# Four-scan phase: merge and gate as two 64-row products, biases from a row of ones

## What is computed

```python
def _s6(x, xw, xb, bcw, bcb, dw, db, yw, yb):
    u = _linear(x, xw, xb)
    bc = _linear(x, bcw, bcb)
    delta = _linear(x, dw, db)
    Bm, Cm = jnp.split(bc, 2, axis=-1)
    A_bar = jnp.exp(-jax.nn.softplus(delta))
    B_bar = (1.0 - A_bar) * Bm
    elems = (A_bar, B_bar * u)
    ...
    _, h = jax.lax.associative_scan(combine, elems, axis=1)
    y = Cm * h
    return _linear(y, yw, yb)
...
y_cat = jnp.concatenate([y1, y2, y3, y4], axis=-1)
y_merged = _linear(y_cat, mw, mb)
gate = jax.nn.sigmoid(_linear(y_cat, gw, gb))
out = _linear(y_merged * gate, ow, ob)
```

## Time and profile before

| | us |
|---|---|
| median of 3 runs | 4187.93 |
| lowest and highest run | 4185.85, 4194.3 |
| profiled execution, its own time | 4188.53 |
| its span, first to last instruction | 4186.8 |
| TensorE, VectorE, ScalarE, GpSimd busy | 3537.3, 2700.7, 2737.2, 1647.8 |
| four-scan phase, from 2602.6 to 3290 of the span | 687.4 |

### The profile page before, as it was taken

The page is one execution under the profiler, slowest core; times in us unless marked ns, Lnnn a source line. Parts: engine busy times, 40 slices in busy tenths (PEclk is TensorE's granted clock), DMA queues, the critical chain, the costliest instruction groups (busy, mean ns, idle before and its releaser), DMA issues. The chain is left out here.

```text
span 4186.8 us, 73185 instructions
## 1 busy us (share of the span) xinstructions
PE 3537.3 (84%) x20680; PEld 2087.7 (50%) x20680; DVE 2700.7 (65%) x4346; ACT 2737.2 (65%) x4888; POOL 1647.8 (39%) x1503
## 2 busy tenths in 40 slices
PE   5899999886778999999976587899998683999946
PEld 2688888643334444444432143444443242999922
DVE  2566666675089999999999375566666573111146
ACT  4455555486988989889864286777776593333346
POOL 0233333200478989889887300455555100000000
PEclk9999999998999999999999798999999896999979
DMA  4000000112566576675752221000000123000022
GB/s 94 22 15 14 15 14 14 24 48 65 140 182 187 139 200 166 176 196 136 204 148 68 73 49 44 16 15 15 16 15 12 27 59 81 6 11 12 12 50 53
DMA packets 208408, 296.61 MB, mean 71 GB/s; under 512 B 73950, under 2 KB 193934, under 8 KB 207506
## 3 DMA queue, kind: packets, MB, share of 16 engines
q1 hardware_dynamic: 199062, 285.59, 26.3%
q10 hardware_dynamic: 9216, 9.65, 1.0%
HBM read 193.01 MB, written 102.03 MB: 70 GB/s over the span
## 5 line engine op out<-in xcount | busy, mean ns | idle before, releaser
L1576 POOL TENSOR_TENSOR mam_hc<-mam_h,mam_cs 128x896 f32<-128x896 f32 x336 | 703.3, 2093 | 181.9 <-DVE mam_h L1541 79.1
L1541 DVE TENSOR_TENSOR_SCAN mam_h<-mam_a,mam_kept,mam_dbx 128x448 f32<-128x448 f32 x672 | 737.5, 1127 | 18.0 <-ACT mam_a L1427 16.9
L1308 PE MATMUL mam_ps_y<-mam_hc,mam_ident 128*128 128x448 f32 x1344 | 568.3, 556 | 130.5 <-POOL mam_hc L1576 130.3
L1962 POOL TENSOR_TENSOR scan_ch<-scan_h,scan_cs 128x392 f32<-128x392 f32 x256 | 348.3, 1376 | 552.4 <-DVE scan_h L1928 552.4
L1308 PEld LDWEIGHTS mam_ps_y<-mam_hc,mam_ident 128*128 128x128 f32 x1344 | 248.4, 192 | 430.8 <-POOL mam_hc L1576 222.3
L1427 ACT ACTIVATE mam_a<-mam_ft,mam_a_neg 128x448 f32<-128x448 f32 x672 | 409.4, 657 | 81.5 <-DVE mam_h L1541 80.7
L1528 DVE TENSOR_TENSOR mam_dbx<-mam_ps_u,mam_bs 128x448 f32<-128x448 f32 x672 | 380.8, 610 | 35.0 <-DMA mam_bs<-dram_bc 35.0
L756 POOL TENSOR_TENSOR att_prob<-att_prob,att_share 128x588 f32<-128x588 f32 x128 | 151.6, 1184 | 452.6 <-DVE att_share L941 452.6
L1928 DVE TENSOR_TENSOR_SCAN scan_h<-scan_turned_in,scan_start 128x392 f32<-128x392 f32 x192 | 252.1, 1330 | 27.9 <-ACT scan_turned_in L1847 26.5
L1802 PE MATMUL scan_ps_merged<-scan_ch,scan_w_merge 128*128 128x392 f32 x512 | 230.7, 532 | 45.6 <-POOL scan_ch L1962 43.6
L2052 PE MATMUL lstm_ps<-lstm_hs,lstm_w_h 128*128 (+1 forms) x1344 | 264.9, 352 | 0.0
(11 more groups left out here) (216 smaller groups left out, 7777.4 us busy)
## 6 DMA issues: line engine op xcount, KB each, us to landing
mam_taps<-normed SPq DMA_DIRECT2D x1008, 43.5 KB
mam_bs<-dram_bc SPq DMA_DIRECT2D x28, 896.0 KB, 14.2
mam_cs<-dram_bc SPq DMA_DIRECT2D x28, 896.0 KB, 16.6
mam_ft<-dram_steps SPq DMA_DIRECT2D x42, 448.0 KB, 4.8
normed<-f_staged SPq DMA_DIRECT2D x384, 38.1 KB
f_mixed<-mixed SPq DMA_DIRECT2D x384, 36.8 KB
dram_gs<-mam_gs SPq DMA_DIRECT2D x56, 224.0 KB, 2.3
mam_gt<-dram_gs SPq DMA_DIRECT2D x56, 224.0 KB, 2.7
```

The source lines that it names most:

```text
L1308: mm = pe.matmul(ps_y[p % 2][:, 0:MT], ident[:], hc[t % 2][:, i, :], start=False, stop=(t % 8 == 7 and i == 1))
L1541: dve.tensor_tensor_scan(h[:, n % 8, :], a[t % 3][:, i, :], dbx[:, i, 0:MT], kept[:, at:at + 1], ALU.mult, ALU.add).then_inc(scanned, 1)
L1576: pool.tensor_tensor(hc[t % 2][:], h[:, row:row + 2, :], cs[:, 2 * pair:2 * pair + 2, :], ALU.mult).then_inc(weighed, 1)
L1962: pool.tensor_tensor(out, hd, in_order(cs, 1 - half, d, t, p), ALU.mult).then_inc(weighed, 1)
```

## The change

- The merge weights become one 128-row tile per direction without zeros: rows 0 to 63 hold merge and gate columns for the first image, rows 64 to 127 gate and merge columns for the second. In place of a product for merge and one for gate over 128 rows, there is a product for each image over its 64 rows. Product 0 leaves merge on partitions 0 to 63 and gate on 64 to 127 of its bank, product 1 the other way round in another bank.
- So the gate activation becomes two of 64 partitions, which read one half of partitions and write the other, and the product with the gate becomes two of 64 partitions.
- A 25th input row of ones in `xin` carries the biases of the four projections. Four small DMAs write it once, and the DMA of the biases is gone.
- u is no longer evacuated. VectorE forms ub = u x rest with u read from PSUM, when the second of three evacuations is done, and drive = B x ub with B read from PSUM.
- C is evacuated by a copy, and TensorE waits for the drive before it projects again.

```diff
-        w_merge = buf.sbuf("w_merge", [P, 2, DIRS, P])
+        w_merge = buf.sbuf("w_merge", [P, DIRS, P])
...
+                for p in range(2):
+                    for image in range(2):
+                        row = 32 * image + C
+                        sp.dma_start(xin[p][row:row + 1], w["rl_ones"][:, 0, 0:ROWS]
+                                     ).then_inc(weights_in, 16)
...
-                        pe.wait_ge(sided, done(c - 1, 4))
-                        pe.wait_ge(multiplied, done(c - 1))
+                        pe.wait_ge(sided, done(c - 1, 3))
+                        pe.wait_ge(fronted, done(c - 1))
...
-                        for a, ps in enumerate((ps_merged, ps_gate)):
-                            mm = pe.matmul(ps[:, 0:N], w_merge[:, a, n, :], ch[p][:, n, :],
+                        for rows, ps in zip((IMAGE_0, IMAGE_1), ps_merged):
+                            mm = pe.matmul(ps[:, 0:N], w_merge[rows, n, :], ch[p][rows, n, :],
                                            start=(n == 0), stop=(n == DIRS - 1))
...
-                    act.activation(gate[p][:], ps_gate[:, 0:N], ACT.Sigmoid,
-                                   bias=merge_b[:, 1:2]).then_inc(sigmoided, 1)
+                    act.activation(gate[p][IMAGE_0], ps_merged[0][IMAGE_1, 0:N], ACT.Sigmoid,
+                                   bias=merge_b[IMAGE_1, 1:2])
+                    act.activation(gate[p][IMAGE_1], ps_merged[1][IMAGE_0, 0:N], ACT.Sigmoid,
+                                   bias=merge_b[IMAGE_0, 1:2]).then_inc(sigmoided, 1)
...
-                        act.wait_ge(projected, done(c - 1, 4) + 1)
-                        act.activation(us[p][:], ps_in[U][:, 0:N], ACT.Identity,
-                                       bias=biases[:, U:U + 1]).then_inc(sided, 1)
...
+                for rows, other in ((IMAGE_0, IMAGE_1), (IMAGE_1, IMAGE_0)):
+                    both = ps_in[0][rows, :].rearrange("i (a d o) -> i a d o", a=2, d=DIRS)
+                    dve.tensor_copy(w_merge[rows, :, rows], both[:, 0])
+                    dve.tensor_copy(w_merge[rows, :, other], both[:, 1])
...
-                    dve.scalar_tensor_tensor(prod[p][:], ps_merged[:, 0:N], merge_b[:, 0:1],
-                                             gate[p][:], ALU.add, ALU.mult).then_inc(gated, 1)
+                    dve.scalar_tensor_tensor(prod[p][IMAGE_0], ps_merged[0][IMAGE_0, 0:N],
+                                             merge_b[IMAGE_0, 0:1], gate[p][IMAGE_0], ALU.add,
+                                             ALU.mult)
+                    dve.scalar_tensor_tensor(prod[p][IMAGE_1], ps_merged[1][IMAGE_1, 0:N],
+                                             merge_b[IMAGE_1, 0:1], gate[p][IMAGE_1], ALU.add,
+                                             ALU.mult).then_inc(gated, 1)
...
+                        dve.wait_ge(sided, done(c - 1, 3) + 2)
+                        dve.tensor_tensor(ub[p][:], ps_in[U][:, 0:N], rest[p][:], ALU.mult
+                                          ).then_inc(multiplied, 1)
+                        dve.wait_ge(multiplied, done(c))
                         dve.wait_ge(projected, done(c - 1, 4) + 3)
-                        dve.wait_ge(sided, done(c, 4))
-                        dve.scalar_tensor_tensor(ub[p][:], ps_in[B_][:, 0:N],
-                                                 biases[:, B_:B_ + 1], us[p][:], ALU.add,
-                                                 ALU.mult).then_inc(multiplied, 1)
-                        dve.wait_ge(multiplied, done(c))
                         dve.tensor_tensor(ring(drive, half)[:, bass.ds((t * 2 + p) * N, N)],
-                                          ub[p][:], rest[p][:], ALU.mult).then_inc(fronted, 1)
+                                          ps_in[B_][:, 0:N], ub[p][:], ALU.mult
+                                          ).then_inc(fronted, 1)
```

More of the change, by code:

```diff
@@ L1664, in four_scan_phase @@
         xin = [buf.sbuf(f"xin{p}", [P, ROWS, PAD]) for p in range(2)]
-        us = [buf.sbuf(f"us{p}", [P, N]) for p in range(2)]
         rest = [buf.sbuf(f"rest{p}", [P, N]) for p in range(2)]
@@ L1680, in four_scan_phase @@
         ps_in = [buf.psum(f"ps_in{i}", [P, BANK]) for i in range(4)]
-        ps_merged = buf.psum("ps_merged", [P, BANK])
-        ps_gate = buf.psum("ps_gate", [P, BANK])
+        ps_merged = [buf.psum(f"ps_merged{image}", [P, BANK]) for image in range(2)]
         ps_out = buf.psum("ps_out", [P, BANK])
@@ L1722, in stages @@
             tail(pairs * K - 1, 1)
+        IMAGE_0, IMAGE_1 = slice(0, LAT), slice(LAT, P)
         def ring(tile, half):
@@ L1738, in _ @@
             def _(sp):
-                for tile, name in ((w_in, "ss_w_in"), (biases, "ss_biases"), (yw, "ss_yw"),
+                for tile, name in ((w_in, "ss_w_in"), (yw, "ss_yw"),
                                    (merge_t, "ss_merge_t"), (yb, "ss_yb"),
@@ L1881, in _ @@
                     dve.memset(small[:, i:i + 1], 0.0).then_inc(sem, 2 * per_chunk)
[L1882 to L1883 removed]
+                dve.memset(start[0][:], 0.0).then_inc(prepared, 1)
+                dve.wait_ge(weights_in, 12 * 16)
                 dve.wait_ge(folded, 1)
                 dve.wait_ge(prepared, 1)
[L1886 to L1891 removed]
+                for rows, other in ((IMAGE_0, IMAGE_1), (IMAGE_1, IMAGE_0)):
+                    both = ps_in[0][rows, :].rearrange("i (a d o) -> i a d o", a=2, d=DIRS)
+                    dve.tensor_copy(w_merge[rows, :, rows], both[:, 0])
+                    dve.tensor_copy(w_merge[rows, :, other], both[:, 1])
                 dve.tensor_tensor(merge_b[:, 0:1], merge_b[:, 0:1], ps_in[1][:, 0:1], ALU.add)
@@ L2208, in four_scan_layout @@
     v = {k[8:]: a[k] for k in a if k.startswith("L2_conv_")}
-    w_in, biases = np.zeros((P, 4, P), f), np.zeros((P, 4), f)
+    w_in = np.zeros((P, 4, P), f)
     mats = (v["xw"], v["dw"], v["bcw"][0:LAT], v["bcw"][LAT:])
@@ L2216, in four_scan_layout @@
             w_in[32 * half:32 * half + C, i, rows] = mats[i].T
-            biases[rows, i] = vecs[i]
+            w_in[32 * half + C, i, rows] = vecs[i]
         w_out[rows, 32 * half:32 * half + C] = v["ow"].T
         b_out[32 * half:32 * half + C, 0] = v["ob"]
-    w["ss_w_in"], w["ss_biases"], w["ss_w_out"], w["ss_b_out"] = w_in, biases, w_out, b_out
+    w["ss_w_in"], w["ss_w_out"], w["ss_b_out"] = w_in, w_out, b_out
     w["ss_yw"] = v["yw"]
```

27 lines of the change are left out of this document (8 added, 19 removed).

## The result

The changed kernel takes 4203.74 us in the median of its runs, the kernel before 4191.83 in the runs beside it: a ratio of 1.0029, with a 95% interval of 1.0018 to 1.0040. It is slower by some 12 us, where the prediction had it faster by 34. Neither sign nor size held.

The account below looks back on a forecast made before the run. The gate-to-gate chain, not TensorE's busy time, was taken as the bound. Slots of 9.55 against 10.08 gave -29.7, with -2.3 - 5 + 2.5 = -34.5 us from 4188.5, then .6 lower for the median: 4153, range 4143 to 4179.

Parts of the forecast that it names:

- The reading of the bound: Four-scan slots: the chain from gate to next gate, 10.08 us on average, sets the time, not TensorE's 525.7 busy of 564.
- Ring: Gate, turned copies, fourth scan, GpSimd's last products, TensorE's last passes, next gate: 4.75 + 1.03 + 2.17 + 1.82 = 9.77 us.
- TensorE's tail: From GpSimd's last product to the next gate: row halves pair, so 1.10 us in place of 1.82.
- (a): Merge products: row halves don't pair, tail stays 1.82, slot 10.27, 4199 us; chance .11.
- (b): Merge products: only half the passes pair, tail about 1.45, slot 9.90, 4176 us; chance .10.
- rival (d): TensorE's clock falls to its lower level in a fifth of the slots, about +1 us on 11, 4165 to 4180; chance .03.
- The second gate: ScalarE: two 64-row gate activations cost one more interval of .48, so the last copy ends at 5.20 instead of 4.72.
- the removed biases give nothing: ScalarE's evacuations: dropping the biases was claimed to cost nothing and give nothing.
- rival (c): VectorE's two gate products are held, .60 to .76 a start; fourth scan ends near 6.55, slot 9.82, 4171 us; chance .14.
- The last 8 slots: Slots that only scan, 9.84 us each before: 9.55 each forecast, 8 x -.29 = -2.3 us.
- The first stage: First 8 slots, which only project: one table load a pair goes, -1.1 us a pair over four pairs, -5 in all.
- The setup: Before TensorE begins: four DMAs for the ones rows, one weight DMA less, and two more VectorE copies, +2.5 us.

Follow-up runs that it names:

- front_copies_first: front_only with ScalarE making the first pair of turned copies ahead of the gate of the slot before; 4135.02 us, ratio .9868 to the kernel before.
- front_only: Kernel before plus ones row and u, B read from PSUM; merge and gate products, gate and product as before; 4175.02 us, ratio .9963.
- before_copies_first: Kernel before with only the first pair of turned copies moved ahead of the gate; 4163.09 us, ratio .9922.
- busy_one: Changed kernel plus one unread TensorE product (.66 us) behind the second direction's merges; 4179.00 us, ratio .9960.
- rows_only: Kernel before plus only the 64-row products per image, two gates and two products with the gate; 4205.32 us, ratio 1.0037.
- after_copies_first: Changed kernel with the first pair of turned copies moved ahead of the gates; 4165.17 us, ratio .9934.
- keep_busy: Changed kernel plus two unread 128-row TensorE products behind the second direction's merges; 4179.59 us, ratio .9972.
- product_split: front_only with only the product with the gate cut into two 64-partition instructions; 4189.04 us, one run.

## Why the prediction was wrong, point by point

**The reading of the bound was right.** Ring and not TensorE's busy time sets the slot: front_copies_first takes .64 a slot off front_only, and before_copies_first .4 off the kernel before, by moving two copies, with no work removed.

**TensorE's tail: right.** Forecast 1.10, measured 1.02 at full clock; the row halves pair. The rule of the Trainium skill (TensorE: Matmul & The Clock Gate, Packing small matmuls) for row groups, of which the trace of before had only the column half, is borne out by these .93 for four passes, and rivals (a) and (b) are out.

**The clock: the step that failed.** I gave rival (d) a chance of .03 and let it reach a fifth of the slots. It reached 33 of 55, at 10.54 - 9.72 = .82 each: 27 us of the 36 between forecast and measurement in this stretch. busy_one, with the clock at 1.00, takes 535.5 for these slots in place of 561.7, so 26 of them come back. The price I put on one slot (1 us) was near; the count and the chance were not. I leaned on the last stage of before, 72% busy at 1.00, against its first stage, which had .90. The busy share doesn't sort these cases: rows_only has 75% and .96, the changed kernel 80% and .90, busy_one 84% and 1.00. A stage that is new (less work, and in 42 of its 55 slots an idle stretch of 1.8 us or more) had no row near it, and I should have given it a large chance. One unread product a slot is enough to keep the clock, and no row of before told on which side of that the new stage would be.

**The second gate: mis-sized.** The step was "the second costs one more interval of .48", since the columns set the time. Its length is indeed .58, but the spacing is .60 and .61: the last copy ends at 2905.36, 5.45 after the gate and not 5.20, and the fourth scan ends at 6.55 and not 6.28. At full clock the slot is 6.55 + 2.15 + 1.02 = 9.72 for the forecast 6.28 + 2.17 + 1.10 = 9.55. That is .17 x 55 = 9 us, the rest of the 36. I also wrote that the removed biases give nothing. That was wrong: the evacuations without a bias take .49 to .51 in place of .58 to .60 and follow each other after .39 in place of .47. It lies off the end of the chain in the changed kernel, and so did not decide.

**The two products, rival (c): happened, and cost nothing.** They are held, .64 and .66, as the Trainium skill (VectorE: DVE Perf Modes, Two Vector instructions with no wait between them) has it, at the low end of the .60 to .76 I gave. The fourth scan ended at 6.55 as (c) said, but for the gates: with only the product cut the slot is 9.84 for 9.79. I put the hold on the wrong engine, and missed it on ScalarE. The second scan starts at 2.51 after the gate (2902.42 - 2899.91) where I had 2.49, but that is luck: the products start at 1.21 and not 1.45, and take .64 and .66 and not .52.

**The last 8 slots**: forecast 76.4, measured 81.1, at a clock of .70. Behind the last gate come 1.2 us more.

**The first stage**: forecast -5 and +2.5, measured -.4 together. One table load a pair is indeed left. But the load that is gone had cost next to nothing: in the trace of before it starts .8 ahead of the projection and ends while that runs. The load that stays was on the path before, and still is: it starts 1.67 behind the start of its projection in the kernel before (2615.63 - 2613.96) and 1.66 behind in the changed one (2627.63 - 2625.97). ScalarE and TensorE in the first stage of the kernel before, then ScalarE and TensorE of the changed one:

```profile
2613.17 1.28 ACT L1860 ACT_TABLE_LOAD   x1
...
2615.63 1.28 ACT L1863 ACT_TABLE_LOAD   x1
...
2613.96 2.87 PE L1790 MATMUL scan_ps_in<-scan_xin,scan_w_in 128*128 128x392 f32 x8 [1.51 <-DVE scan_ub L1937]
```

```profile
2627.63 1.28 ACT L1865 ACT_TABLE_LOAD   x1 [2.33 <-PE scan_ps_in L1793]
2628.93 0.50 ACT L1865 ACTIVATE scan_decay<-scan_ps_in 128x392 f32 x1
```

```profile
2621.82 2.87 PE L1793 MATMUL scan_ps_in<-scan_xin,scan_w_in 128*128 128x392 f32 x8 [1.25 <-DVE scan_drive L1943]
2625.97 2.87 PE L1793 MATMUL scan_ps_in<-scan_xin,scan_w_in 128*128 128x392 f32 x8 [1.27 <-DVE scan_drive L1943]
2631.37 4.36 PE L1793 MATMUL scan_ps_in<-scan_xin,scan_w_in 128*128 128x392 f32 x8 [2.54 <-DVE scan_drive L1943]
```

A pair at full clock takes 9.55, against 9.69 in the earlier trace rows: -.14 and not -1.1. The step that failed is "of the two loads, 2.57, I take .9 to lie on the path of the slot that has them". One projection more than before was lengthened by the lower clock (4.36 for 2.87), 1.5. The setup cost .6 from the phase's start to the first projection and not 2.5. From the first projection of the stage to the one behind it the stage took .5 longer, and from there to the first gate 1.5 less.

**The sum again.** 55 slots: -27.7 forecast, +9.4 for the gates, +27.1 for the clock: +8.8, and 561.7 - 553.0 = +8.7 is measured. With +1.6, +1.2 and -.4 for the rest this is +11.1.

## What to carry to other kernels

Work taken from TensorE beside an unchanged ring turns into idle time, and here the idle time cost some 26 us through the clock. Where a change opens idle stretches in every turn of a loop, ask what the turn costs at the lower clock and give that case a real chance; and before giving up on such a change, try one unread product in the gap. Cutting ScalarE's gate in two by partitions cost a whole instruction and the overlap with the next (.72), not one more spacing (.48); the same cut on VectorE, which had time to spare, cost .05. Look first at the engine that waits before the link of the ring: moving two copies into that wait was worth 40 us on top of the front half, and 28 on the kernel before by the phase, where the front half alone was worth 16.

## What the runs showed of the hardware that I had not expected

- A clock of .90 at 80% busy and of 1.00 at 84%, with the same chain of work: the only difference is .66 us of unread work a slot. What decides between them stays open: busy share alone does not, since rows_only has .96 at 75%; the longest idle stretch alone does not either, since after_copies_first, at .96, has none over 1.0 in 54 of its 55 slots, and busy_one and keep_busy, at 1.00, have some of 1.2. The last 8 slots stayed at .98 to 1.00 in the four kernels with one gate and one product, and fell to .70 to .92 in all others: before has 1.00 at 72% busy, product_split .91 at 75%.
- In one kernel slots with the same idle stretch of 1.8 us before the third merge are long or short by turns, as the clock falls in them or not.
- Two activations on opposite partition halves follow each other at the full length of each (.60 for .58), where one of 128 partitions is followed after .48.
- A phase whose code is untouched took 1358 to 1380 us over fourteen traces. The span of one trace against another's says nothing below some 20 us; the length of the changed phase repeated to 5.
